# Causal softmax: dividing the probabilities in SBUF instead of scaling the turned output

## The reference, cut to what matters

```
h = layernorm(x)*(1+ca)+sa
x = x + ga * attention_1(h)     # sliding window of 128, RoPE, sinks in the denominator
h = layernorm(x)*(1+cb)+sb
y = h + attention_2(rmsnorm(h)) # causal, 32 heads on 8 key/value heads
x = x + gb * (y + moe(rmsnorm(y)))
```

## Time and profile before

| | |
|---|---|
| time, three runs | 1060.79, 1061.67, 1062.79 us; median 1061.67 |
| profiled execution, span from first to last instruction | 1063.1 us |
| PE busy | 965.1 us (91%) |
| DVE busy | 789.4 us (74%) |
| ACT busy | 753.5 us (71%) |
| POOL busy | 466.7 us (44%) |
| causal half | 422 to 812 us of the span |

### The profile page before, as it was taken

One profiled execution on the slowest core, in us unless ns is written; L12 is line 12 of the kernel. 1 busy time (PEld: TensorE's weight loads), 2 busy tenths in 40 slices (PEclk: granted clock), 3 DMA queues, 4 the chain that ended last, 5 costly groups with the idle time before them and its releaser, 6 DMA issues.

```text
span 1063.1 us, 22951 instructions
## 1 busy us (share of the span) xinstructions
PE 965.1 (91%) x6862; PEld 901.5 (85%) x6862; DVE 789.4 (74%) x2308; ACT 753.5 (71%) x2122; POOL 466.7 (44%) x550
## 2 busy tenths in 40 slices
PE   5589999999899899999999999999998589999991
PEld 3379899998789799988999999999887489999991
DVE  6779998989899577777777777777764756666646
ACT  3368788887888688788888778877884346555641
POOL 4346668777656333433444332232222852222243
PEclk8899999999999899999999999999997699999996
DMA  8799879787476675465557455354303365555313
GB/s 178 185 233 274 208 190 276 209 213 201 112 177 147 167 190 155 122 164 135 136 140 166 122 168 120 110 153 126 71 1 120 115 221 172 166 170 162 103 58 116
DMA packets 146059, 166.18 MB, mean 156 GB/s; under 512 B 79194, under 2 KB 100714, under 8 KB 140816
## 3 DMA queue, kind: packets, MB, share of 16 engines
q1 hardware_dynamic: 129440, 143.58, 52.0%
q0 software_dynamic: 3712, 11.16, 3.3%
q10 hardware_dynamic: 12784, 9.97, 3.0%
HBM read 105.88 MB, written 58.79 MB: 155 GB/s over the span
## 4 chain that ended last, share of the span: by engine, by line
PE 56%; DVE 17%; issue 10%; ACT 9%; DMA 4%; POOL 1%; SPq 1%; DVEq 0%; ACTq 0%; POOLq 0%
PE psO L1086 14%; PE psS L1053 10%; PE psX L1063 8%; PE psY L1102 6%; PE psP L985 6%; ACT wgt_hi L1319 3%; DVE pbuf L1734 2%; DVE gated L2074 2%; DVE pTl L1756 2%; PE psO L1069 2%; PE psS L1236 2%; PE psP L998 2%; ACT relu_s L1624 2%; PE psX L1236 1%; DVE den L1748 1%
## 5 line engine op out<-in xcount | busy, mean ns | idle before, releaser
L1351 ACT ACTIVATE pbuf<-pbuf,nmax 128x256 f32<-128x256 f32 (+3 forms) x512 | 264.9, 519 | 45.8 <-DVE nmax L1734 44.7
L1053 PE MATMUL psS<-kT,qE 128*128 128x256 f32 (+3 forms) x1024 | 238.2, 317 | 25.7 <-DVE nmax L1734 24.1
L1734 DVE CUSTOM_DVE_ANT_0 pbuf<-psS,mcau 128x256 f32<-128x256 f32 (+3 forms) x512 | 219.9, 435 | 46.9 <-PE psS L1053 41.0
L1756 DVE TENSOR_TENSOR pTl<-psX,pTh 128x512 fp32r<-128x512 f32 x272 | 187.1, 688 | 73.5 <-ACT pTh L1319 72.9
L1319 ACT ACTIVATE pTh<-psX 128x512 fp32r<-128x512 f32 x272 | 160.7, 591 | 55.7 <-PE psO L1086 39.3
L1053 PEld LDWEIGHTS psS<-kT,qE 128*128 128x128 f32 x1024 | 160.2, 192 | 40.3 <-DVE nmax L1734 33.7
L1086 PE MATMUL psO<-pTh,vpad 128*128 128x256 f32 x1088 | 187.1, 294 | 3.2 <-DVE oS L1762 2.0
L798 POOL TENSOR_TENSOR ol<-oS,oh 128x256 fp32r<-128x256 f32 x128 | 94.8, 741 | 200.7 <-ACT oh L1319 196.2
L1063 PE MATMUL psX<-idn,pbuf 128*128 128x128 f32 x1088 | 162.2, 274 | 3.1 <-DVE pTl L1756 3.1
L1086 PEld LDWEIGHTS psO<-pTh,vpad 128*128 128x128 f32 x1088 | 150.3, 190 | 10.5 <-DVE oS L1762 5.4
L1063 PEld LDWEIGHTS psX<-idn,pbuf 128*128 128x128 f32 x1088 | 126.5, 141 | 9.4 <-DVE pTl L1756 3.3
(11 more groups left out here) (295 smaller groups left out, 2369.0 us busy)
## 6 DMA issues: line engine op xcount, KB each, us to landing
qd<-st SPq DMA_DIRECT2D x32, 1024.0 KB, 4.5
qE<-qd SPq DMA_DIRECT2D x128, 256.0 KB, 6.0
mrawV<-in_w_moe SPq DMA_DIRECT2D x32, 384.0 KB
mrawB<-in_w_moe SPq DMA_DIRECT2D x32, 384.0 KB
kT<-kd SPq DMA_DIRECT2D x64, 128.0 KB, 4.4
kT<-kd SPq DMA_DIRECT2D x32, 256.0 KB, 4.3
kd<-st SPq DMA_DIRECT2D x7, 1024.0 KB, 4.8
xg<-sq ACTq DMA_DIRECT2D x7, 640.0 KB, 6.1
```

Of the source, the lines that this page charges most:

```text
L1053: last = mm(psS[j % 2][:, 0:n], qE[:, g % 2, j, t * P:(t + 1) * P], kT[:, g % 2, c, k0:k0 + n], start=(c == 0), stop=(c == 1))
L1351: nc.scalar.activation(pj, pj, ACT.Exp, bias=nmax[:, u % 4, j:j + 1], scale=-1.0, accum_out=sums[:, u % 4, j:j + 1]).then_inc(a_exp, 1)
L1734: V.tensor_tensor_reduce(probs(u, j), psS[j % 2][:, 0:n], mcau[:, SEQ - n:], -SCALE, 3e38, ALU.add, ALU.min, nmax[:, u % 4, j:j + 1]).then ...
L1756: V.tensor_tensor(pTl[:, kt % 2, :], psX[kt % 2][:, :], pTh[:, kt % 2, :], ALU.subtract).then_inc(v_pl, 1)
```

## The change

In the causal units the probabilities themselves are multiplied by the reciprocal, before they are turned, and so psO holds the finished output. VectorE divides heads 0, 1 and 2 of a unit, in place in pbuf; ScalarE divides head 3. `turn_probs(u, 0)` now waits for both. `denominator(u)` moves one step earlier. `spread`, `turn_scale`, `scale_of` and `scale_out` fall away for these units. `out_hi` reads psO, and the low part is taken from psO by VectorE (`out_lo`) in the place of GpSimd's `out_low`. `out_project` runs one step earlier (for u-4) and stands in front of `turn_probs(u-2, 1)`, no longer at the step's end. Windowed units keep the old way. The core of the diff:

```diff
+W = 2 * SEGU
@@ TensorE
             def turn_probs(u, k):
                 kt = KT[u] + k + 1
                 if k == 0:
-                    pe.wait_ge(a_exp, QM * (u + 1))
+                    if windowed(u):
+                        pe.wait_ge(a_exp, QM * (u + 1))
+                    else:
+                        pe.wait_ge(v_norm, u - W + 1)
+                        pe.wait_ge(a_norm, u - W + 1)
             def values(u, k):
                 if k == 0:
-                    wait(pe, v_os, u)
+                    wait(pe, v_os, min(u, W))
+                    wait(pe, v_ol, u - W)
             def out_project(u):
-                pe.wait_ge(g_ol, u + 1)
+                if windowed(u):
+                    pe.wait_ge(g_ol, u + 1)
+                else:
+                    pe.wait_ge(v_ol, u - W + 1)
@@ TensorE step_causal
-                if u - 3 < NU:
+                if u - 3 < W:
                     turn_scale(u - 3)
+                if u < W + 5:
+                    out_project(u - 5)
+                if W + 4 <= u < NU + 4:
+                    out_project(u - 4)
                 if nk > 1:
                     turn_probs(u - 2, 1)
...
                 if nk > 3:
                     turn_probs(u - 2, 3)
-                out_project(u - 5)
                 if nk > 3:
                     values(u - 2, 2)
@@ ScalarE
+            def divide(u):
+                act.wait_ge(v_rden, u + 1)
+                last = probs(u, QM - 1)
+                nc.scalar.activation(last, last, ACT.Copy, scale=rden[:, u % 4, QM - 1:QM]).then_inc(a_norm, 1)
             def out_hi(u):
-                act.wait_ge(v_os, u + 1)
+                if windowed(u):
+                    act.wait_ge(v_os, u + 1)
+                else:
+                    act.wait_ge(s_PV, KT[u + 1])
                 wait(act, s_Y, u - 1)
-                copy(oh[:, u % 2, :], oS[:, u % 2, :]).then_inc(a_oh, 1)
+                copy(oh[:, u % 2, :], oS[:, u % 2, :] if windowed(u) else psO[:, 0:2 * P]).then_inc(a_oh, 1)
@@ ScalarE step_causal
                     exp_head(u, 0)
-                if u - 3 < NU:
+                if u - 4 < W:
+                    out_hi(u - 4)
+                if u - 3 < W:
                     scale_of(u - 3)
+                elif u - 3 < NU:
+                    out_hi(u - 3)
...
                 if nk > 3:
                     probs_hi(u - 2, 3)
+                if W <= u - 1 < NU:
+                    divide(u - 1)
                 if now:
                     exp_head(u, 3)
-                if u - 4 < NU:
-                    out_hi(u - 4)
@@ VectorE
+            def divide(u):
+                dve.wait_ge(v_rden, u + 1)
+                for j in range(QM - 1):
+                    last = V.tensor_scalar(probs(u, j), probs(u, j), rden[:, u % 4, j:j + 1], None, ALU.mult)
+                last.then_inc(v_norm, 1)
+            def out_lo(u):
+                dve.wait_ge(a_oh, u + 1)
+                V.tensor_tensor(ol[:, u % 2, :], psO[:, 0:2 * P], oh[:, u % 2, :], ALU.subtract).then_inc(v_ol, 1)
@@ VectorE step_causal
-                if u - 3 < NU:
+                if u - 3 < W:
                     scale_out(u - 3)
-                if u - 2 < NU:
+                elif u - 3 < NU:
+                    out_lo(u - 3)
+                if u == W:
                     denominator(u - 2)
+                if W <= u - 1 < NU:
+                    denominator(u - 1)
+                    divide(u - 1)
+                elif u == W:
+                    denominator(u - 1)
                 if nk > 1:
                     probs_lo(u - 2, 1)
```

More of the change, by code:

```diff
@@ L374, in build @@
         v_rden = sem("v_rden")
+        v_norm = sem("v_norm")
+        v_ol = sem("v_ol")
+        a_norm = sem("a_norm")
         v_pl = sem("v_pl")
@@ L831, in step @@
                 seg, r = divmod(u, SEGU)
-                if 0 <= u - 4 < NU:
+                if 0 <= u - 4 < W:
                     out_low(u - 4)
@@ L843, in step @@
                     rope_sum(ahead(u)[:2])
-                if 0 <= u - 1 < NU:
+                if 0 <= u - 1 < W:
                     spread(u - 1)
@@ L1201, in _ @@
             pe.wait_ge(v_pl, KT[NU])
-            pe.wait_ge(v_os, NU)
+            pe.wait_ge(v_ol, NU - W)
             for t in range(TB, NT):
```

## The result

The changed kernel takes 1090.43 us (median of 4 runs, 1087.88 to 1090.98) against 1061.72 for the kernel before (4 runs): ratio 1.0271, interval 1.0251 to 1.0290. It is 28.7 us slower; 16.9 were forecast. Direction and mechanism were right, the size was short by 11.8 us. 1090.4 lies at the lower edge of the band that the forecast gave to rival C (1090 to 1112), just above its own (1068 to 1090).

A forecast was written before the change was run, and what follows sets the result against it. TensorE was taken to set the pace, busy 380.67 of 390.00 us in the causal half. New waits of 36.8 less 13.4, 2.5 and 4.0 gave +16.9 us, so 1079 us, range 1046 to 1099.

The forecast's parts named there:

- rival C: Causal half: VectorE's multiplies collide with GpSimd's work, losing 20 us more; 1099 us, band 1090 to 1112, chance 0.13.
- What goes: Causal half: removed turn_scale saves TensorE 13.4 us, half its idle time 2.5; other removed work counts only at attention's end.
- The end: End of attention: the last output product ends near 809.4 us, 4.0 us less, bounds 2 and 5.
- (a): Boundary into step t = 1: turn_probs waits 0.94 us for ScalarE's divide; 12.6 us over 15 boundaries.
- (c): Boundary into step t = 3: the transposes wait 0.5 to 0.7 us for a divide; 10.1 us together.
- (d): Boundary into step t = 0: the transposes wait 0.38 us with K, Q or feature items; 5.7 us together.
- (b): Inside step t = 1: values(u-2, 2) waits 0.56 us for probs_lo(u-2, 2); 8.4 us in 15 steps.
- As a total it fits: VectorE in the causal half: 72 us of multiplies make 351 of 390 us busy, still under TensorE's 381 - 13.
- Rival B: A draw: half of the chains hidden, say (c) and (d); +1.1 us, 1063 us, band 1056 to 1067, chance 0.10.
- Rival A: Faster: all waits at the four boundaries covered; -19.9 us, 1042 us, band 1038 to 1056, chance 0.17.

The follow-up runs named there:

- the last GpSimd run: Changed kernel with output product late, GpSimd dividing heads 2 and 3, VectorE head 0, ScalarE head 1 early: 1067.3 us, ratio 1.006 to the kernel before.

## Why the prediction was right, and where its size was short

The direction and the places of the waits were right; that 1090.4 still falls inside 1046 to 1099 is owed to the width that the rivals gave the range. The runs split the 47.3 us between the undivided kernel with its output product late (1043.2) and the changed one (1090.4): 16.7 for moving the product, 24.3 more for ScalarE's divide, 6.3 more for VectorE's. The forecast has 36.8 of new waits on a base of 1041.8. The kernel before took 1060.6 beside the undivided runs and 1061.7 beside the changed one, so about 1 us of the split is not to be trusted.

- **What goes: right.** 1060.6 to 1043.2 is -17.4; the forecast has -13.4 - 2.5 - 4.0 = -19.9. The end is the smaller part of it: the row-to-row distance shrank by 3.6 us, but where the last two units alone were changed, only 0.7 us reached the median, which noise covers. The profile of the kernel before had a stretch behind attention of 249.7 us, and those of the thirteen changed kernels 243.5 to 246.2; with one execution of the kernel before that does not make a gain.
- **(a), (c), (d): right in place and count, (c) and (d) short in size.** Start to start, less the undisturbed pair, TensorE waits in the changed kernel 12.0 us at (a), 15.8 at (c) and 8.7 at (d), where the forecast has 12.6, 10.1 and 5.7. Without VectorE's multiplies it is 14.1, 14.3 and 8.7: 37.1 for 28.4. Three terms come to about these 8.7 us. ScalarE's divide was priced by the plain copy at 0.31 to 0.62 us and takes 0.39 to 0.72 with the scale of a [P, 1] column: 0.09 to 0.10 on each of 46 chains, 4.2 us. The waking of TensorE was put at 0.05 us and takes 0.10 on each chain: 2.3 us. The two steps with a table load are another 2.3 us longer than their like; the forecast had no such term.
- **(b): right**, 0.56 us in most steps, but about half of it in three with a V item: 7.8 us for 8.4. The scores behind nmax that the moved product also brings (5.2 us) were not foreseen; in the changed kernel (0.8 us) the waits at the boundaries cover them.
- **VectorE: the step that was wrong is to price it by "As a total it fits".** Its total was right (67 for 72 us). But in a list in order the multiplies delay the low parts and maxima behind them. They cost 6.3 us on top of ScalarE's late divide, and 16.1 where they are the only divide (1059.9 to 1076.0). The forecast counted VectorE only at (c) without item, 3.0 us; these five steps came to 4.9, and without the multiplies ScalarE held them for 3.2.
- **Rival C: the mechanism is there, its price was too high here.** Collisions took 5.1 us of VectorE's time, not 20. With the multiplies moved early in the step, where GpSimd's subtractions run, they took 19.7. The Trainium skill's rule ("SBUF — State Buffer", section "Who interferes with whom"), that the second comer is blocked while the first one's instruction lasts, agrees with the 1.37 us row, which starts 0.20 us after GpSimd's and ends 0.28 us after it.
- **Rival B** had (c) and (d) hidden; they are the two that came out longest against the forecast.
- **Rival A** is what the undivided run with the late product shows, 1043 for 1042: the gain is real. The moved product alone eats it (1059.9), and so do the divides alone (1076 to 1077).

One thing stays open: with cover and place both mended, the divides still cost 33 us (1043.2 to 1076 or 1077), and how much of this is VectorE's and how much ScalarE's was not separated there: no run leaves out one engine's divide alone with the output product late.

## What to carry to other kernels

Here an operation moved onto engines "with idle time" cost what the operations behind it in their lists lost, not what its total added; look at what is queued behind it and which engine waits for that. Before moving a block of work within the busiest engine's list, ask which chains it covered where it stood: this one, worth 0.72 us per step, covered four. And price work by leaving it out: two parts that hide each other cost 24.3 and 16.1 us alone, and 30.5 together.

## What the runs showed of the hardware

- ScalarE's copy with a per-partition scale takes 0.09 to 0.10 us more than the plain copy at the same width (721 ns at 512 columns for 625, 497 at 256 for 408).
- TensorE's transposes started 0.10 us after the end of ScalarE's divide, in each of the 46 waits of the run without VectorE's multiplies.
- VectorE's multiply by a [P, 1] column, SBUF to SBUF, takes 0.28 to 0.48 us alone and up to 1.6 us while GpSimd has an operation running (the longest in the last GpSimd run). GpSimd's own takes 0.6 to 1.65 us for 128 to 512 columns.
- In the changed kernel TensorE's waits for ScalarE's divide appear in the trace as "issue", with no releaser; moving the divide early took 17.9 of the 19.8 us away, and leaving it out all of them. That is not so in every kernel: where GpSimd has two heads and the others one, the trace names ScalarE:

```profile
PE psX L1083 <- ACT pbuf L1400: 4.2, 6, 1.2
```
